# A two-block graph network on one core: the last attention block turned to rows on partitions, and a front with W·a on GpSimd, two casts on ScalarE and LayerNorm's scales a step later

## The reference

```python
h = relu(layernorm(x))
# first graph block
s = adj @ h
attn_a = sigmoid(concat([s, h]) @ Wa.T + ba);  attn_b = sigmoid(concat([s, h]) @ Wb.T + bb)
g = h @ W_sa
scores = (g @ a_sa[:256])[:, None] + (g @ a_sa[256:])[None, :]
e = where(adj != 0, exp(-leaky_relu(scores, 0.01)), 0)
x_a = (e / (e.sum(1) + 1e-5)) @ g
x_b = adj @ (h @ W_gcnb) + b_gcnb
x = x + sigmoid(attn_a * x_a + attn_b * x_b)
# second block, two attention layers
h = relu(layernorm(x))
for l in range(2):
    Wh, Ws = split(h @ W_stack[l])
    a = softmax(Wh @ Ws.T) * adj          # softmax over all columns, then the mask
    h = leaky_relu(a @ Wh + h, 0.01)
out = x + h
```

## Time and profile before

| | |
|---|---|
| runs | 1616.38 us median of 3 (1614.1 to 1616.49) |
| the profiled execution | 1616.64 us; span from first to last instruction 1614.8 us; mean granted clock 0.995 |
| busy, share of the span | PE 96%, DVE 71%, ACT 66%, POOL 61% |
| instructions | 34761 |

### The profile page before, as it was taken

One profiled execution on the slowest core, in us unless ns is written; L12 is line 12 of the kernel. 1 busy time (PEld: TensorE's weight loads), 2 busy tenths in 40 slices (PEclk: granted clock), 3 DMA queues, 4 the chain that ended last, 5 costly groups with the idle time before them and its releaser, 6 DMA issues.

```text
span 1614.8 us, 34761 instructions
## 1 busy us (share of the span) xinstructions
PE 1555.8 (96%) x12902; PEld 1540.1 (95%) x12902; DVE 1152.6 (71%) x2165; ACT 1071.4 (66%) x2090; POOL 982.6 (61%) x874
## 2 busy tenths in 40 slices
PE   5999999999999999999999999999999999999984
PEld 5999999999999999999999999999999999999984
DVE  7766766666665677777777777756777777777774
ACT  3579898988985566666666666646666666666663
POOL 2112222222220488888888888837888888888896
PEclk9999999999999999999999999999999999999998
DMA  4124444454441133333333335513333333333332
GB/s 147 40 53 118 118 119 117 119 149 114 117 105 33 40 98 100 99 98 99 99 99 99 100 101 178 173 46 86 99 99 99 102 103 99 104 101 99 99 109 68
DMA packets 88666, 163.36 MB, mean 101 GB/s; under 512 B 9265, under 2 KB 19376, under 8 KB 88240
## 3 DMA queue, kind: packets, MB, share of 16 engines
q1 hardware_dynamic: 60624, 113.41, 24.1%
q0 software_dynamic: 24336, 44.31, 11.2%
q10 hardware_dynamic: 3536, 3.41, 0.6%
HBM read 147.99 MB, written 13.11 MB: 100 GB/s over the span
## 4 chain that ended last, share of the span: by engine, by line
PE 80%; issue 6%; DVE 5%; POOL 5%; ACT 2%; DMA 0%; POOLq 0%; SPq 0%; DVEq 0%; ACTq 0%
PE PS L1133 29%; PE PS L1341 8%; PE PS L1344 8%; PE PS L1343 8%; PE PS L1208 5%; PE PS L1205 5%; PE PS L1207 5%; PE PS L1204 5%; PE PS L1206 5%; POOL FR L435 2%; POOL X L428 2%; DVE AF L957 1%; ACT FR L596 1%; DVE AF L930 1%; DVE PS L997 1%
## 5 line engine op out<-in xcount | busy, mean ns | idle before, releaser
L1133 PE MATMUL PS<-FR,RB 128*128 128x256 f32 x4056 | 536.6, 281 | 1.8 <-ACT X L578 1.8
L435 POOL TENSOR_TENSOR FR<-AF,FR 128x512 fp32r<-128x512 f32 x338 | 450.8, 1334 | 129.4 <-ACT FR L596 129.3
L1133 PEld LDWEIGHTS PS<-FR,RB 128*128 128x128 f32 x4056 | 500.9, 188 | 3.1 <-ACT X L578 3.0
L428 POOL TENSOR_TENSOR X<-X,ROW 128x512 f32<-128x512 f32 x294 | 384.8, 1309 | 82.3 <-ACT ROW L606 82.3
L1341 PE MATMUL PS<-FR,RA 128*128 128x256 f32 x1352 | 388.6, 287 | 18.8 <-POOL FR L435 18.2
L1344 PE MATMUL PS<-FR,RA 128*128 128x256 f32 x1352 | 379.7, 281 | 0.0
L1343 PE MATMUL PS<-FR,RA 128*128 128x256 f32 x1352 | 378.8, 280 | 0.0
L957 DVE TENSOR_TENSOR AF<-PS,AJ 128x512 f32<-128x512 f32 x338 | 231.7, 685 | 82.5 <-ACT PS L590 81.0
L1341 PEld LDWEIGHTS PS<-FR,RA 128*128 128x128 f32 x1352 | 254.4, 188 | 27.9 <-POOL FR L435 25.5
L401 POOL DMA_DIRECT2D STGT<-adjt x169 | 90.1, 534 | 296.1 <-PE PS L1208 296.1
L1343 PEld LDWEIGHTS PS<-FR,RA 128*128 128x128 f32 x1352 | 254.7, 188 | 0.0
(11 more groups left out here) (142 smaller groups left out, 2329.4 us busy)
## 6 DMA issues: line engine op xcount, KB each, us to landing
AJ<-adjt SPq DMA_DIRECT2D x338, 256.0 KB, 2.7
STGT<-adjt POOLq DMA_DIRECT2D x169, 256.0 KB, 3.0
xt_scratch<-ROW SPq DMA_DIRECT2D x12, 512.0 KB, 2.6
RB<-xt_scratch SPq DMA_DIRECT2D x12, 512.0 KB, 4.5
x_scratch<-X ACTq DMA_DIRECT2D x13, 256.0 KB, 2.2
ROW<-x_scratch SPq DMA_DIRECT2D x13, 256.0 KB, 3.1
out<-ROW SPq DMA_DIRECT2D x12, 256.0 KB, 3.3
X<-xt SPq DMA_DIRECT2D x1, 1536.0 KB, 11.3
```

The lines of the kernel that those rows point to most:

```text
L428: nc.gpsimd.tensor_tensor(slot, slot, MB.unsqueeze(1).broadcast_to([P, 2, 256]), ALU.subtract)\
L435: nc.gpsimd.tensor_tensor(LO[g % 2], WA[g % 2], HI[g % 3].bitcast(F32), ALU.subtract)\
L1133: last = nc.tensor.matmul(out, stationary(a, k), moving(b, k), start=(k == 0 and i == 0), stop=(k == K - 1 and i == 2))
```

## The change

It has two parts that share no instruction.

**Last attention block (b = 25, units g from GL = 325).** Its scores are computed with rows on partitions and columns along the free dimension (stationary and moving operand exchanged). A row's maximum is then a maximum along the free dimension: `maximum` keeps the running maximum over all units, `last_max` reduces it to one column per half and negates it. `row_exponent` does exponent, subtraction (as the activation's bias) and sum (as its accumulated output) in one ACT instruction per half, in place in the ring slot. PE's `turn_last` transposes the slot into the bank that `exponent` used to write, two steps ahead of the weighing; `mask`, `high` and `low` follow as before. `weigh_last` exchanges the operands, so that the result has rows on partitions in bank 5. `subtract`, `exponent`, `total`, the folds, turns and spreads, `weighted`, `residual`, `leaky`, `turn_out` and `result` of this block are gone; `join_rows`, `turn_rows` and `keep_rows` bring x into rows beforehand, `last_sum` and `last_result` close.

**Front.** The two products of W·a and the memset of WX's padding go to POOL, between its first two `inverse_root`; the high casts of WSL and WX go to ACT, between `transposed_high(0)` and the loop; on DVE the first sum stands ahead of `scales(1)`, the second behind `normalise(1)`. In the loop, `scales` of a group leaves the end of pair p and comes after `transposed_low` of the next.

```diff
+LB = LAYERS * PAIRS - 1
+GL = UNITS * LB
-S_END = {s_step(UNITS * b + UNITS - 1): b for b in range(LAYERS * PAIRS)}
-A_END = {a_step(UNITS * b + UNITS - 1): b for b in range(LAYERS * PAIRS)}
+S_END = {s_step(UNITS * b + UNITS - 1): b for b in range(LB)}
+A_END = {a_step(UNITS * b + UNITS - 1): b for b in range(LB)}
+A_ALL = A_END | {a_step(NG - 1): LB}
...
             inverse_root(0, *LN_PARTS[0])
+            pool.wait_ge(w_in, 16)
+            nc.gpsimd.memset(WRAW0[:, :, GX + D + 3:WC], 0.0).then_inc(wv_zero, 1)
+            pool.wait_ge(row_in, 16)
+            for side in range(2):
+                nc.gpsimd.tensor_tensor(PEB[:, :, 0:D] if side == 0 else PAB[:, :, 0:D],
+                                        WRAW0[:, :, GX:GX + D],
+                                        AROW[:, side * D:(side + 1) * D].unsqueeze(1).broadcast_to([P, K, D]),
+                                        ALU.mult).then_inc(wv_pool, 1)
             inverse_root(1, *LN_PARTS[1])
...
-                if y is not None:
+                if y is not None and y < GL:
                     subtract(y)
...
             transposed_high(0)
+            act.wait_ge(wv_step, 1)
+            nc.scalar.activation(WSL[:, 0, :, :], WV[:, 0, :].unsqueeze(2).broadcast_to([P, K, P]), ACT.Copy)\
+              .then_inc(wsl_hi, 1)
+            act.wait_ge(wv_step, 3)
+            act.wait_ge(wv_zero, 1)
+            nc.scalar.activation(WX[:, 0, :, GX:WC], WRAW0[:, :, GX:WC], ACT.Copy).then_inc(wh_cast, 1)
...
+            def row_exponent(g):
+                u, slot = g % UNITS, RING[g % SLOTS]
+                n = 255 if u == UNITS - 1 else 256
+                act.wait_ge(nmax_d, 1)
+                act.wait_ge(ev_d, g + 1)
+                for h in range(2):
+                    e = slot[:, h * 256:h * 256 + n]
+                    last = nc.scalar.activation(e, e, ACT.Exp, bias=NMX[:, h:h + 1], accum_out=ESUM[:, h, u:u + 1])
+                last.then_inc(lexp_d, 1)
...
-                if x is not None:
+                if x is not None and x < GL:
                     exponent(x)
...
                 if x is not None:
                     high(x)
+                z = A_AT.get(v + 3)
+                if z is not None and z >= GL:
+                    row_exponent(z)
+                if v == a_step(GL) + 2:
+                    keep_rows()
...
-            dve.wait_ge(row_in, 16)
-            for side in range(2):
-                nc.vector.tensor_tensor(...)
+            dve.wait_ge(wv_pool, 1)
+            nc.vector.reduce_sum(WV[:, 0, :], PEB[:, :, 0:D], AX).then_inc(wv_step, 1)
             scales(1, 2, 6)
             normalise(1)
+            dve.wait_ge(wv_pool, 2)
+            nc.vector.reduce_sum(WV[:, 1, :], PAB[:, :, 0:D], AX).then_inc(wv_step, 1)
...
             for p in range(PAIRS):
                 if 1 <= p < PAIRS - 1:
                     transposed_low(p + 1)
+                if p - 1 in LN_CHAIN:
+                    i = LN_CHAIN[p - 1]
+                    scales(i, *LN_PARTS[i])
...
                 if p in LN_CHAIN:
                     i = LN_CHAIN[p]
                     variances(i, *LN_PARTS[i], 2 + sum(b <= LN_PARTS[i][1] for a, b in LN_STATS.values()))
-                    scales(i, *LN_PARTS[i])
...
+            def last_max():
+                dve.wait_ge(max_d, NG)
+                dve.wait_ge(bcm_d, LB)
+                nc.vector.reduce_max(MXC, RM.rearrange("p (h j) -> p h j", h=2), AX).then_inc(lmax_d, 1)
+                dve.wait_ge(lmax_d, 1)
+                nc.vector.tensor_scalar(NMX, MXC, -1.0, None, ALU.mult).then_inc(nmax_d, 1)
...
+            def last_result():
+                dve.wait_ge(av_mm, NG)
...
+                for h in range(2):
+                    last = nc.vector.scalar_tensor_tensor(YROW[:, h, :], PS[:, 5, h * D:(h + 1) * D], RC[:, h:h + 1],
+                                                          XROW[:, h, :], ALU.mult, ALU.add)
+                last.then_inc(yrow_d, 1)
+                dve.wait_ge(yrow_d, 1)
+                nc.vector.scalar_tensor_tensor(YROW, YROW, SLOPE, YROW, ALU.mult, ALU.max).then_inc(yleak_d, 1)
...
+                nc.vector.tensor_tensor(to, YROW, to, ALU.add).then_inc(res_d, 1)
...
+                if e == NG - 1:
+                    last_max()
-                if x is not None:
+                if x is not None and x < GL:
                     total(x)
...
+                if v == a_step(GL) + 1:
+                    join_rows()
+                if v == a_step(NG - 1) - 1:
+                    last_sum()
+                if v == a_step(NG - 1) + 1:
+                    last_result()
...
+            def turn_last(g):
+                n = g - GL
+                pe.wait_ge(lexp_d, n + 1)
+                pe.wait_ge(mask_d, g - 1)
+                if n < 2:
+                    pe.wait_ge(sum_d, g - 1)
+                for jj in range(2):
+                    for h in range(2):
+                        last = nc.tensor.transpose(PS[:, 2 + g % 2, jj * 256 + h * P:jj * 256 + (h + 1) * P],
+                                                   RING[g % SLOTS][:, h * 256 + jj * P:h * 256 + (jj + 1) * P],
+                                                   IDN[:, :])
+                last.then_inc(tl_mm, 1)
...
+                z = A_AT.get(v + 2)
+                if z is not None and z >= GL:
+                    turn_last(z)
+                if v == a_step(GL) + 2:
+                    turn_rows()
-                if a is not None:
+                if a is not None and a < GL:
                     weigh(a)
+                elif a is not None:
+                    weigh_last(a)
```

More of the change, by code:

```diff
@@ L271, in two_graph_blocks @@
         res_d = sem("res_d")
+        lmax_d = sem("lmax_d")
+        nmax_d = sem("nmax_d")
+        lexp_d = sem("lexp_d")
+        tl_mm = sem("tl_mm")
+        lsum_d = sem("lsum_d")
+        lrec_d = sem("lrec_d")
+        xsum_d = sem("xsum_d")
+        tx_mm = sem("tx_mm")
+        xrow_d = sem("xrow_d")
+        yrow_d = sem("yrow_d")
+        yleak_d = sem("yleak_d")
         out_stored = sem("out_stored")
@@ L930, in maximum @@
                     nc.vector.tensor_tensor(RM, PS[:, g % 2, :], RM, ALU.max).then_inc(max_d, 1)
+                elif g >= GL:
+                    rm, s = (t.rearrange("p (h j) -> p h j", h=2)[:, :, 0:255] for t in (RM, PS[:, g % 2, :]))
+                    nc.vector.tensor_tensor(rm, s, rm, ALU.max).then_inc(max_d, 1)
                 else:
@@ L949, in row_max, with last_sum, join_rows @@
                   .then_inc(rmax_d, 1)
+            def last_max():
[4 more added lines that the diff above has]
+                nc.vector.tensor_scalar(NMX, MXC, -1.0, None, ALU.mult).then_inc(nmax_d, 1)
+            def last_sum():
+                dve.wait_ge(lexp_d, UNITS)
+                dve.wait_ge(bcr_d, LB)
+                nc.vector.reduce_sum(DC, ESUM[:, :, :], AX).then_inc(lsum_d, 1)
+                dve.wait_ge(lsum_d, 1)
+                nc.vector.reciprocal(RC, DC).then_inc(lrec_d, 1)
+            def join_rows():
+                dve.wait_ge(lmax_d, 1)
+                nc.vector.tensor_tensor(XSUM, XT[:, PAIRS - 1, 0, :, :].bitcast(F32),
+                                        XT[:, PAIRS - 1, 1, :, :].bitcast(F32), ALU.add).then_inc(xsum_d, 1)
+            def last_result():
+                n = PAIRS - 1
+                dve.wait_ge(av_mm, NG)
+                dve.wait_ge(lrec_d, 1)
+                dve.wait_ge(xrow_d, 1)
+                dve.wait_ge(t5_mm, PAIRS - 1)
+                for h in range(2):
[4 more added lines that the diff above has]
+                nc.vector.scalar_tensor_tensor(YROW, YROW, SLOPE, YROW, ALU.mult, ALU.max).then_inc(yleak_d, 1)
+                dve.wait_ge(yleak_d, 1)
+                dve.wait_ge(x1r_in[n % 2], 16 * (n // 2 + 1))
+                to = X1R[:, n % 2, :, :]
+                nc.vector.tensor_tensor(to, YROW, to, ALU.add).then_inc(res_d, 1)
             def mask(g):
                 b, u = g // UNITS, g % UNITS
-                dve.wait_ge(exp_d, g + 1)
+                if g < GL:
+                    dve.wait_ge(exp_d, g + 1)
+                else:
+                    dve.wait_ge(tl_mm, g - GL + 1)
                 dve.wait_ge(adj_full[g % NADJ], 16 * (g // NADJ + 1))
@@ L1345, in weigh, with weigh_last, turn_rows @@
                 last.then_inc(av_mm, 1)
+            def turn_last(g):
[10 more added lines that the diff above has]
+                last.then_inc(tl_mm, 1)
+            def weigh_last(g):
+                u = g % UNITS
+                if u == 0:
+                    pe.wait_ge(y2_d, LB - 1)
+                pe.wait_ge(alo_d, g + 1)
+                for jj in range(2):
+                    j = 2 * u + jj
+                    for h in range(2):
+                        i0 = jj * 256 + h * P
+                        hi, lo = HI[g % 3][:, i0:i0 + P], LO[g % 2][:, i0:i0 + P]
+                        to = PS[:, 5, h * D:(h + 1) * D]
```

(14 more changed lines are left out.)

46 lines of the change are left out of this document (26 added, 20 removed).

## The result

The changed kernel takes 1598.25 us, median of 5 runs (1597.79 to 1599.32), against 1616.38 for the kernel before in 5 runs beside it (1614.1 to 1617.77). The ratio is 0.9894, with a 95% interval of 0.9883 to 0.9904. The forecast was 1599.1.

A forecast was written before the change was run, and what follows sets the result against it. TensorE, busy 96% of the span, bounds the body, so only start and end could pay: span 1614.8-6.4-10.8 = 1597.6, plus 1.84 over the span, less 0.26 to the median, gives 1599.1 us; range 1597 to 1606.

The forecast's parts named there:

- A: Whole kernel: front and last block both gain as priced, 1599.1 us, own range 1597 to 1602; chance 0.73.
- B: TensorE between 17 and 47 us: its clock still falls, the front gives half, 3 us; about 1602; chance 0.15.
- E: Last block: summing exponent makes ScalarE change its function table, two loads a unit, 28 us; 1627; chance 0.02.
- the front: Start and loop over pairs: 4.9 plus 1.5 of clock, 6.4 us faster, bounds 3.5 and 7.5.
- W·a and the casts: Kernel start: work leaves VectorE, its last split of W ends 1.39 us earlier, `products_l(0)` near 15.6.
- The scales: Loop over pairs: `scales` behind `transposed_low` shortens TensorE's stalls and keeps its clock at 44 us; 5.0 us.
- The pace: Steady units of the last block: TensorE becomes the bound, 1.86 us a unit instead of 2.49.
- The entry: Start of the last block: weigh_last(327) at 1573.9 instead of 1575.20, 1.3 us gained.
- The tail: Last matmul to the end of the last addition: 2.35 us instead of 5.07, gain 2.7.
- The end as a whole: Last block through the last addition: 8.1 plus 2.7, 10.8 us faster, bounds 7 and 11.5.
- C: Last block: ScalarE becomes the bound, summing exponents at 1.0 each, 2.55 us a unit; 1606; chance 0.08.
- D: Last block: transposes cost TensorE its clock, 3.4 us a unit at 1.2 GHz; about 1617; chance 0.02.

The follow-up runs named there:

- run 9: The kernel before, unchanged, profiled once more: 1614.52 us in one execution.
- run 5: The changed kernel with each transpose of the last block's slots made twice, 4 more a unit: 1603.12 us in one execution.
- Run 7: The changed kernel with mask(326) ahead of weighted(24) on VectorE: 1596.99 us in one execution.
- run 1: The kernel before with only the last block of the change, front as before: 1605.47 us, ratio 0.9936.
- run 2: The kernel before with only the front's changes, old last block: 1610.26 us, ratio 0.9967.
- run 4: The kernel before with only `scales` moved behind `transposed_low` of the next pair: 1611.47 us, ratio 0.9974.
- run 6: The changed kernel with one more ScalarE copy of 128x512 added to every unit of the last block: 1601.11 us in one execution.
- run 10: The changed kernel with the 12 matmuls of each weigh_last replaced by 24 transposes: 1613.41 us in one execution.
- run 8: The changed kernel with the statistics of pairs 1, 3 and 4 behind the low half of the next pair: 1598.52 us in one execution.
- run 11: The changed kernel with mask(326) ahead of weighted(24), statistics of pairs 1, 3 and 4 behind the next low half, last store's second half from ScalarE: 1598.12 us.
- run 3: The kernel before with only W·a's products on GpSimd and the casts on ScalarE: 1612.84 us, ratio 0.9983.

## Why the prediction was right, point by point

The time (1598.25 against 1599.1) and the mechanism of A are right: both stages gave nearly what they were priced at, and none of B to E took place. That the front came so near is partly luck: two of its terms were off in opposite directions.

- **W·a and the casts.** Given 1.39, with `products_l(0)` near 15.6. It came at 15.90, 1.14 earlier, since ScalarE's cast started at 14.47 instead of 14.20. The prediction took that for the whole of the part. It brought 1.0 more between there and the marker, which the prediction put at nothing: it did not see that the matmuls up to 22 us ran at the pace of 1.2 GHz (2.80 for twelve at 18.48). For the same reason its remark in B, that the stalls before 27 did not make the clock fall, holds for the one of 2.14 at 26.79 only; after the wait of 1.97 at 16.62 in run 9 it did fall.
- **The scales.** Given 5.0 (the 6.4 less 1.39), of it 1.5 of clock; 4.5 to 4.7 from start to marker. Right in place, and size to within 10%: `products_h(3)` at 37.03 (37.7 given) with 0.20 of wait; the new stall near 45.5 came at 45.03 with 0.91 (1.0 to 1.2); the stall at pair 6 went. The clock stayed at full speed at 44 us in every kernel without the long stall. The front gave 6.6 to 6.8 against 6.4, W·a 0.7 over its price and the scales 0.3 under.
- **The pace.** 1.86 given, 1.86 measured, and run 5 shows that TensorE sets it. ScalarE's pair cost 1.0, as taken.
- **The entry**, the mis-sized term of the end: 1.3 given, 0.8 measured, `weigh` of 327 at 1565.95 (with the 8.45 of shift, 1574.40) against the 1573.9 given. The step had the inverse sums of block 24 late on ScalarE, and four operations ahead of mask(327) on VectorE. It did not join the two: `weighted(24)`, one of VectorE's four, waits for those sums, mask(326) stands behind it, and `high`, the next exponent and TensorE's turn of 328 stand behind that, 1.67 in all. Run 7 took 0.8 of it away by an order alone.
- **The tail.** 2.7 given, 2.7 measured (5.07 to 2.37). The stores after it took 8.19 (8.14).
- **The end as a whole:** 10.8 given, 10.2 in the profile and 10.1 in run 1.
- **Left out of the sum:** the slow stretch behind the marker. The span was forecast at 1597.6 and was 1596.2; the stretch makes 1.44 of that, and the terms' own errors (the front 0.4 more, 0.2 more up to the last maximum, the end 0.6 less) nearly cancel.

B is refuted by runs 2 and 4, C by run 6 (0.35 of room remained), D by run 10, and E by the pace and by the groups of the changed kernel, which still have one load of a table in all:

```profile
L559 ACT ACT_TABLE_LOAD x1 | 1.3, 1283 | 0.8 <-PEq L1612 0.8
```

## What to carry to other kernels

A kernel that is 96% busy on one engine still pays at its ends: find the stage where that engine waits, name the engine that sets the pace there, and move work until the busy engine itself is the bound; the gain a unit is then the difference of two slot sums, which can be read from the trace before. When walking an order by hand at a seam, follow each operation's own waits too, not only the work ahead of it in its queue. And compare stages between markers, not only whole times: a slow stretch of the clock of 1.45 us that comes and goes is as large as most of the single edits here. A stage's sum can also be right by terms that are off both ways, as the front's was.

## What the runs showed of the hardware

- **A slow stretch that comes and goes.** Behind the marker, where TensorE waits once, 1.96 us at the change of stages (at 111.39 before, 104.59 in the changed kernel), the granted clock fell to 0.50 for a few microseconds in 6 of 14 profiles (the kernel before once of two, runs 1, 2, 8, 10 and 11) and stayed at 1.00 in the other 8. It costs 1.45 us each time (89.0 against 87.6). Kernels with the same front, such as the changed one and run 10, fell on both sides, so it isn't the front's work. What decides it stays open. In contrast, the stall of 2.7 us before `products_h(3)` was followed by the clock of 0.50 in each of the four profiles that have it, and no profile without it has a slow stretch there. The length of a stall alone doesn't decide it either: 2.71 before 26.36 in run 9 and 3.03 before 25.12 in run 3 were followed by twelve matmuls in 1.73 at 1.00.
- **The start of the clock.** The six matmuls of `products_l(0)` took 1.65 at 17.04 in the kernel before and 0.98 at 16.62 in its second profile, so the time at which the clock first rises differs between executions of one kernel. In the second the clock fell again at 17.9, for 4 us. Whether by a late rise or by a fall, `products_h(0)` ran slowly in all four profiles with the old start and in none of the ten with the new one, where TensorE waits 0.5 to 0.8 ahead of `products_l(0)` instead of 1.8 to 2.1.
- **A summing exponent** on ScalarE adds an instruction of its own, ACTIVATION_READ_ACCUMULATOR, 0.19 long and 0.09 in the slot. The table is not loaded anew.
- **Transposes** of 128x128 of fp32 follow each other at 0.109, hardly less than the 0.118 of this kernel's matmuls, which have twice the columns, and in run 10 they held the full clock alone.
- **A store on a second queue** didn't end earlier in the one profile that has it: 8.75 us from the last addition to the end of the span, against 8.2 with both behind each other on SyncE.
